# A fused attention and Hadamard-FFN block on one core: mixing W_down's blocks on GpSimd instead of TensorE, W_down loaded once, and new instruction orders

## The chip, the cores and the metric

One core of a Trainium2 chip. The metric is the device time of the whole kernel in microseconds (us), the median of several runs; lower is better.

## The reference, cut to what matters

The block runs over 8 sequences of 512 tokens and width 512. After the attention half comes a feed-forward half whose inputs are rotated by a Walsh-Hadamard transform (`fwht`) along the feature axis:

```python
x = x + layernorm(attention(layernorm(x)))       # 16 heads of 32, softmax, W_o
n = layernorm(x)
h = fwht(n * SU_ug) / 64                         # transform over 512
u = h @ W_up.T   * (Wscale_ug[:2048] * 64)
g = h @ W_gate.T * (Wscale_ug[2048:] * 64)
h = silu(g) * u
h = fwht(h * SU_dp) / 64                         # transform over 2048
x = x + layernorm(h @ W_down.T * (Wscale_dp * 64))
```

The transform is linear and symmetric, so it can be applied to the weights once instead of to the activations of every sequence. W_down is 512 x 2048, so its transform runs over 2048 = 16 blocks of 128. A Hadamard matrix of 2048 is one of 16 (it mixes the blocks, with signs) times one of 128 (it mixes inside a block).

## The kernel before

All matmuls are fp16 with each fp32 value split into a high and a low half; a product takes three passes (high-high, high-low, low-high). Work falls into three stages.

**Front.** Loads, the split of the attention weights (`asl`, `ash`), and the transform of the three FFN weights, interleaved with the attention of sequence 0 and part of that of sequence 1. **Steady cycle.** Six times the same list: the FFN of one sequence interleaved with the attention of the next. **Back.** What is left.

The order in each engine's queue is written out by hand-made lists: `FRONT` once and `ORDER` for each cycle, one string per engine (PE, ACT, DVE, POOL, SP). A token such as `smax.0.3` calls the function `smax` with those arguments; `@1` means for the next sequence, `@-1` for the one before. A planner wrote the lists; the hardware only sees the semaphore waits inside the functions. The work slots in PSUM (`MIDDLE`, `UPPER`) belong to the lists.

The steps that the change and the prediction touch, with their lines:

- SP: `ldx.k` (L573) loads 1 MB chunk k of W_down (k 0 to 3), W_up (4 to 7) and W_gate (8 to 11) to look for its largest value; `raw.k` (L586) loads the same chunk again to split it. `ln1.t` (L634) transposes token tile t of the normalized input, `stk` and `stq` (L656) the k and q tiles.
- DVE: `mx.k` takes the largest value of a chunk (L1150), `dmx`/`dsc` work out W_down's scale (`d_scaled`), `smax` takes the row maximum of scores (L1403).
- ACT: `ash` (L962, L964) scales and rounds attention weights, `cut.k` (L992, L1000) scales and rounds chunk k, `dyh`, `dzh`, `ue`, `uhh` copy PSUM results out, `exp`, `exr`, `exq` are the softmax exponentials.
- POOL: `asl` (L1482) and `cut.k` (L1486) subtract to get the low halves; `proj` and `tok` (L1504, L1509) finish the rotary embedding before `stk`; `xn` (L1498) the low half of the input.
- PE: `c`, `proj`, `v`, `smax`, `st`, `av`, `o` are the attention; `gate`, `up` (L913) and `down` (L938) the FFN; `warm.n` (L697) are n matmuls whose result nobody reads.
- The transform of W_down: `dy.n` (L738) transposes four blocks and sums them with signs (32 matmuls of 128 columns): the mixing over the low two bits of the block number. `dz.n` (L750, in `mixed`) multiplies by the 128-Hadamard and mixes over the high two bits: 4 blocks x 2 halves = 8 matmuls of 512 columns. There are 16 of each. `dyh`/`dyl` and `dzh`/`dzl` take the results out of PSUM, `dst` stores them.
- The transform of W_up and W_gate: `ut` (L764) and `uh` (L750), 32 of each.

The first `dy` waits for all four `cut` chunks: `pe.wait_ge(cut_lo, 4)`.

Of the kernel before, what the change touches and what calls it, by code (L numbers as in the profile page):

```python
# [44 lines left out]
ROW_SHIFT = 2.0 ** 12  # L45

# [15 lines left out]
        up.7@-1 smax.2.5 smax.2.6 gate.8@-1 smax.2.7 smax.2.8 smax.2.9 up.8@-1 st.22 gate.9@-1 st.23 smax.2.10  # L62
        av.2.0 proj.3.0 st.24 av.2.1 down.6@-1 st.25 down.7@-1 smax.2.11 smax.2.12 down.8@-1 smax.2.13 smax.2.14
        smax.2.15 up.9@-1 st.26 proj.3.1 st.27 gate.10@-1 up.10@-1 st.28 gate.11@-1 st.29 up.11@-1 gate.12@-1
        st.30 st.31 up.12@-1 st.32 av.3.0 av.3.1 st.33 down.9@-1 st.34 gate.13@-1 up.13@-1 st.35 st.36
        down.10@-1 smax.3.0 down.11@-1 st.37 st.38 gate.14@-1 up.14@-1 st.39 av.4.0 smax.3.1 smax.3.2 smax.3.3
        down.12@-1 smax.3.4 av.4.1 smax.3.5 c.1@1 gate.15@-1 st.40 smax.3.6 up.15@-1 c.0@1 down.13@-1 smax.3.7
        smax.3.8 down.14@-1 st.41 smax.3.9 smax.3.10 down.15@-1 st.42 smax.3.11 proj.0.0@1 gate.16@-1 st.43
        smax.3.12 smax.3.13 up.16@-1 smax.3.14 smax.3.15 gate.17@-1 proj.0.1@1 st.44 st.45 up.17@-1 gate.18@-1
        up.18@-1 st.46 gate.19@-1 st.47 up.19@-1 av.5.0 av.5.1 gate.20@-1 st.48 st.49 st.50 up.20@-1 gate.21@-1  # L70
        st.51 down.16@-1 down.17@-1 smax.0.0@1 smax.0.1@1 smax.0.2@1 up.21@-1 st.52 proj.1.0@1 smax.0.3@1
        smax.0.4@1 down.18@-1 down.19@-1 st.53 smax.0.5@1 smax.0.6@1 gate.22@-1 st.54 st.55 st.56 up.22@-1
        av.6.0 av.6.1 st.57 smax.0.7@1 down.20@-1 smax.0.8@1 down.21@-1 smax.0.9@1 smax.0.10@1 smax.0.11@1
        gate.23@-1 st.58 st.59 up.23@-1 gate.24@-1 st.60 up.24@-1 st.61 st.62 gate.25@-1 up.25@-1 proj.1.1@1
        st.63 av.7.0 down.22@-1 down.23@-1 smax.0.12@1 smax.0.13@1 gate.26@-1 smax.0.14@1 smax.0.15@1 down.24@-1
        av.7.1 v.0@1 v.1@1 up.26@-1 v.2@1 v.3@1 gate.27@-1 up.27@-1 st.0@1 st.1@1 gate.28@-1 up.28@-1 st.2@1
        down.25@-1 st.3@1 o.0 st.4@1 smax.1.0@1 gate.29@-1 o.1 st.5@1 up.29@-1 smax.1.1@1 smax.1.2@1 down.26@-1
        down.27@-1 o.2 smax.1.3@1 st.6@1 gate.30@-1 st.7@1 av.0.0@1 up.30@-1 proj.2.0@1 gate.31@-1 up.31@-1
        smax.1.4@1 smax.1.5@1 down.28@-1 av.0.1@1 smax.1.6@1 smax.1.7@1 smax.1.8@1 down.29@-1 o.3 down.30@-1
        down.31@-1 smax.1.9@1 smax.1.10@1 gate.0 up.0 gate.1 st.8@1 up.1 st.9@1 gate.2 smax.1.11@1 proj.2.1@1  # L80
        up.2 smax.1.12@1 st.10@1 smax.1.13@1 gate.3 up.3 st.11@1 smax.1.14@1 smax.1.15@1 down.0 st.12@1 st.13@1
# [1511 lines left out]
```

## Time and profile before

| what | us |
|---|---|
| median of 3 runs | 1946.56 (1945.4 to 1946.8) |
| the profiled execution | 1942.76 |
| its span, first to last instruction | 1940.8 |
| TensorE busy | 1842.3 (95%) |
| VectorE busy | 1276.8 (66%) |
| ScalarE busy | 1159.5 (60%) |
| GpSimd busy | 940.2 (48%) |
| mean granted TensorE clock | 0.991 of full |

Times in the views are from the start of the span. PE is TensorE, PEld its weight load, DVE VectorE, ACT ScalarE, POOL GpSimd, SPq the queue from which SyncE issues DMAs. A busy PE is not PE at its peak: the ends of matmuls are modelled and overlap the next ones, so the price of a group of matmuls is read from the starts, or from the chain.

### The profile page before, as it was taken

The page shows a single profiled execution, that of the slowest core. Times are in us where ns is not written, and L with a number is a line of the kernel's source. Part 1 is how long each engine was busy: PE and PEld are TensorE (multiplying, and loading weights), DVE is VectorE, ACT ScalarE, POOL GpSimd, SP SyncE. Part 2 cuts the span into 40 slices and gives each one's busy share as a digit, 9 for nine tenths or more (in the row PEclk, how much of TensorE's full clock was granted, in tenths as well). Part 3 has the DMA queues.
Part 4 walks back from the last instruction along what each step waited for, and adds up shares of the span by engine and source line. Part 5 has one row for each costly group of instructions (what it writes and reads, how often), then busy time and mean ns, then how long its engine had stood idle before and what let it go on. Part 6 is the DMA issues. An engine that isn't in the chain of part 4 may idle for free.

```text
span 1940.8 us, 46270 instructions
## 1 busy us (share of the span) xinstructions
PE 1842.3 (95%) x18248; PEld 1286.9 (66%) x18248; DVE 1276.8 (66%) x2669; ACT 1159.5 (60%) x2003; POOL 940.2 (48%) x990
## 2 busy tenths in 40 slices
PE   3699989999999999999999999999999999999998
PEld 1366555777667676767667776767677767777775
DVE  8788566776677766776677666776677666664322
ACT  3568998665647654666556564666457655664222
POOL 3624554464456444555456444545456445444322
PEclk9899999999999999999999999999999999999999
DMA  8745432463346325463455333543556334522422
GB/s 250 246 115 139 130 77 55 121 126 72 88 120 134 73 73 137 108 123 77 109 126 131 72 91 101 141 76 80 127 124 121 72 93 113 117 70 75 136 76 76
DMA packets 351959, 213.15 MB, mean 110 GB/s; under 512 B 284160, under 2 KB 285440, under 8 KB 350720
## 3 DMA queue, kind: packets, MB, share of 16 engines
q1 hardware_dynamic: 343536, 198.72, 43.1%
q10 hardware_dynamic: 8208, 11.48, 1.9%
q8 instruction: 146, 2.39, 0.5%
q14 instruction: 69, 0.57, 0.1%
HBM read 122.06 MB, written 20.98 MB: 74 GB/s over the span
## 4 chain that ended last, share of the span: by engine, by line
PE 76%; DVE 8%; ACT 5%; issue 4%; POOL 3%; DMA 2%; SPq 1%; POOLq 0%; ACTq 0%; DVEq 0%
PE ps L913 29%; PE ps L938 15%; PE ps L849 5%; PE ps L839 4%; PE ps L860 4%; PE ps L905 4%; PE ps L871 4%; PE ps L750 3%; DVE mx L1403 2%; PE ps L808 2%; PE ps L874 2%; ACT p_hi L1089 2%; POOL p_lo L1516 1%; PE ps L738 1%; PE ps L818 1%
## 5 line engine op out<-in xcount | busy, mean ns | idle before, releaser
L1089 ACT ACTIVATE p_hi<-ps,exp_scale 128x512 f16<-128x512 f32 x512 | 352.1, 688 | 232.1 <-PE ps L860 228.5
L1516 POOL TENSOR_TENSOR p_lo<-p,p_hi 128x512 f16<-128x512 f32 x256 | 296.5, 1158 | 259.5 <-ACT p L1095 246.0
L1403 DVE TENSOR_REDUCE mx<-ps 128x1 f32<-128x512 f32 x512 | 331.5, 684 | 120.3 <-PE ps L849 118.0
L913 PE MATMUL ps<-x2T,gate_w 128*128 128x256 f16 x3072 | 377.5, 273 | 8.5 <-DVE room L1451 8.4
L913 PE MATMUL ps<-x2T,up_w 128*128 128x256 f16 x3072 | 377.4, 273 | 0.0
L938 PE MATMUL ps<-room 128*128 128x512 f16 x1536 | 363.4, 379 | 0.1
L1544 POOL TENSOR_TENSOR room<-room 128x256 f16<-128x256 f32 x256 | 171.9, 672 | 380.5 <-ACT room L1125 379.1
L913 PEld LDWEIGHTS ps<-x2T,gate_w 128*128 128x128 f16 x3072 | 297.6, 98 | 67.1 <-DVE room L1451 14.8
L913 PEld LDWEIGHTS ps<-x2T,up_w 128*128 128x128 f16 x3072 | 299.1, 98 | 48.0 <-issue 3.0
L1418 DVE TENSOR_TENSOR p_lo<-ps,p_hi 128x512 f16<-128x512 f32 x256 | 175.8, 687 | 171.2 <-ACT ps L1100 99.6
L938 PEld LDWEIGHTS ps<-room 128*128 128x128 f16 x1536 | 148.2, 97 | 163.8 <-issue 3.0
L1120 ACT ACTIVATE room<-ps,half_gate 128x256 f32<-128x256 f32 x256 | 119.5, 473 | 154.8 <-PE ps L913 148.6
L1449 DVE SCALAR_TENSOR_TENSOR room<-room,ps 128x256 f32<-128x256 f32 x256 | 106.1, 414 | 153.0 <-ACT room L1120 152.2
L1095 ACT ACTIVATE p<-ps,exp_scale 128x512 f32<-128x512 f32 x256 | 176.2, 688 | 16.4 <-POOL p_lo L1516 16.4
L849 PE MATMUL ps<-kT,qT 96*128 96x512 f16 x512 | 163.8, 387 | 20.9 <-DVE mx L1403 7.0
L860 PE MATMUL ps<-qT,kT 128*128 128x256 f16 x1024 | 175.4, 273 | 5.2 <-DVE mx L1403 3.9
L1125 ACT ACTIVATE room<-room 128x256 f16<-128x256 f32 x256 | 105.1, 417 | 118.8 <-DVE room L1451 60.0
L1100 ACT ACTIVATE ps<-ps,exp_scale 128x512 f32<-128x512 f32 x256 | 169.7, 663 | 6.3
L860 PEld LDWEIGHTS ps<-qT,kT 128*128 128x128 f16 x1024 | 94.1, 98 | 48.4 <-DVE mx L1403 8.5
L1423 DVE RECIPROCAL nsc<-ps 128x256 f32<-128x256 f32 x64 | 112.0, 1750 | 21.1 <-PE ps L874 19.8
L1489 POOL TENSOR_TENSOR rs<-ve,mhalf 128x1 f32<-128x1 f32 x128 | 73.3, 576 | 94.2 <-DVE ve L1355 94.2
L1504 POOL TENSOR_TENSOR ra<-ra,rb 128x512 f32<-128x512 f32 x64 | 81.2, 1268 | 73.0 <-DVE rb L1394 58.2
(197 smaller groups left out, 2580.9 us busy)
## 6 DMA issues: line engine op xcount, KB each, us to landing
room<-down_mid SPq DMA_DIRECT2D x256, 256.0 KB, 3.0
xr<-in_x SPq DMA_DIRECT2D x34, 256.0 KB, 3.4
y_mid<-xr SPq DMA_DIRECT2D x32, 256.0 KB, 2.6
room<-y_mid ACTq DMA_DIRECT2D x32, 256.0 KB, 3.4
xa<-in_x SPq DMA_DIRECT2D x30, 256.0 KB, 3.2
out<-room SPq DMA_DIRECT2D x24, 256.0 KB, 2.1
x2T<-in_W_gate SPq DMA_DIRECT2D x5, 1024.0 KB, 6.1
gate_w<-in_W_down SPq DMA_DIRECT2D x4, 1024.0 KB, 7.1
```

Of the source, the lines that this page charges most:

```text
L849: nc.tensor.matmul(work[k], qT[0:STACK, g % 2, t, h, :], kT[0:STACK, g % 2, :, h, :], start=True, stop=True).then_inc(sm_filled.sem, 1)
L860: mm = nc.tensor.matmul(work[k][:, hh * HALF:(hh + 1) * HALF], kT[:, g % 2, kt, 2 * j + hh, :], qT[:, g % 2, 2 * qh:2 * qh + 2, 2 * j + hh ...
L913: mm = nc.tensor.matmul(ffn_ps[i % 2][:, half * HALF:(half + 1) * HALF], weights[:, chunks[j // 4], kt, pw, j % 4 * P:(j % 4 + 1) * P], x2 ...
L938: mm = nc.tensor.matmul(down_ps[t], hid[:, i % 2, ph, t * P:(t + 1) * P], wr[:, i % WB, pw, :], start=j == n == 0, stop=j == NJ - 1 and n ...
L1089: nc.scalar.activation(hi_buf(b, U)[:, 2 * j:2 * j + 2, :].rearrange("p h q -> p (h q)"), work[k], ACT.Exp, scale=exp_scale[:, 0:1]).then_ ...
L1095: nc.scalar.activation(p32[:], work[k], ACT.Exp, scale=exp_scale[:, 0:1]).then_inc(p_right.sem, 1)
L1100: nc.scalar.activation(work[k], work[k], ACT.Exp, scale=exp_scale[:, 0:1]).then_inc(p_left.sem, 1)
L1120: nc.scalar.activation(act[:, i % 2, :], ffn_ps[i % 2][:, 0:HALF], ACT.Tanh, scale=half_gate[:, 0:1]).then_inc(tanh_done.sem, 1)
L1403: nc.vector.tensor_reduce(mx[:, t, h:h + 1], work[k], AX.X, ALU.max).then_inc(sm_freed.sem, 1)
L1418: nc.vector.tensor_tensor(lo, work[k], hi, ALU.subtract).then_inc(st_freed.sem, 1)
L1516: nc.gpsimd.tensor_tensor(lo, p32[:], hi, ALU.subtract).then_inc(p_low.sem, 1)
L1544: nc.gpsimd.tensor_tensor(hid[:, i % 2, 1, :], act[:, i % 2, :], hid[:, i % 2, 0, :], ALU.subtract).then_inc(h_lo.sem, 1)
```

## The change

- The mixing over the high two bits of the block number is done by `bf.k` on GpSimd, in fp32, on the raw chunk as it was loaded: two butterfly steps over runs of 512 and 1024 columns, each one addition and one subtraction of 128 x 1024, out of place into `mid` and back. `dz` keeps only the 128-Hadamard: 2 matmuls in place of 8, and each `dz` needs only its own `dy`.
- W_down's chunks are loaded once, into the room of the later `up_w`; `mx` reads them there. `ldx.0` to `ldx.3` are gone. `bf.k` may overwrite the chunk only after `mx.k`.
- Two buffers of `raw`, `cut` and `turned` and their waits are rearranged, and all lists, `MIDDLE` and `UPPER` are written anew by the planner with other durations. The steady cycle is a rotation of the same tokens in a new order; `FRONT` ends a few tokens later.

```diff
+MIX = (4 * P, 8 * P)
...
-        RAW_AT = [gate_part(2), gate_part(0), gate_part(1), gate_part(2), gate_part(0), gate_part(2), gate_part(0), gate_part(2),
-                  x2_16, gate_part(0), x2_16, x2_16]
+        RAW_AT = [up_part(c) for c in range(4)] + [gate_part(0), x2_16, gate_part(0), x2_16, gate_part(0), x2_16, x2_16, x2_16]
+        mid = gate_part(3).bitcast(F32)
...
             def dz(b, n):
-                pe.wait_ge(t_done, 4 * (n // 4) + 4)
-                mixed(n, n % 4)
+                pe.wait_ge(t_done, n + 1)
+                if n == 0:
+                    pe.wait_ge(bo_sum, 2)
+                if n >= 2:
+                    pe.wait_ge(q_done, n - 1)
+                for i in range(2):
+                    mm = nc.tensor.matmul(ps[:, 6 + n % 2, :], had[0], d_turned[:, n % 2, i, :], start=i == 0, stop=i == 1)
+                mm.then_inc(q_filled, 1)
...
+            def bf(b, k):
+
+                pool.wait_ge(d_in[k], 16)
+                for n, width in enumerate(MIX):
+                    src, dst = ((raw[k], mid), (mid, raw[k]))[n % 2]
+                    left, right = (src.rearrange("p (m i n) -> p m i n", i=2, n=width)[:, :, i, :] for i in range(2))
+                    both = dst.rearrange("p (m i n) -> p m i n", i=2, n=width)
+                    if n == 0 and k:
+                        pool.wait_ge(d_mixed, k)
+                    if n:
+                        pool.wait_ge(d_turn, (len(MIX) - 1) * k + n)
+                    if n == 1:
+                        pool.wait_ge(m_seen, k + 1)
+                    nc.gpsimd.tensor_tensor(both[:, :, 0, :], left, right, ALU.add)
+                    nc.gpsimd.tensor_tensor(both[:, :, 1, :], left, right, ALU.subtract).then_inc(
+                        d_mixed if n == len(MIX) - 1 else d_turn, 1)
```

The `cut` of ScalarE waits for the mixing, and `dy` for the four W_down cuts under their own semaphore:

```diff
             def cut_(b, k):
-                sc.wait_ge(r_loaded[k % 3], 16 * (k // 3 + 1))
-                sc.wait_ge(d_scaled if k < 4 else f_scaled, 1)
+                if k < 4:
+                    sc.wait_ge(d_mixed, k + 1)
+                    sc.wait_ge(d_scaled, 1)
...
                 if n == 0:
-                    pe.wait_ge(cut_lo, 4)
+                    pe.wait_ge(d_lo, 4)
```

The beginning of three of the new lists, against the old (cut):

```diff
 FRONT POOL
-        xs.0 xs.1 xn.0 xs.2 xs.3 xn.1 xn.2 xn.3 asl.0 asl.1 asl.2 asl.3 asl.4 asl.5 asl.6 asl.7 asl.8 proj.0.0
-        asl.9 tok.0.0 asl.10 asl.11 proj.0.1 xs.0@1 tok.0.1 cut.0 proj.1.0 xs.1@1 tok.1.0 cut.1 cut.2 cut.3
+        xs.0 xs.1 xs.2 xn.0 xn.1 xs.3 bf.0 xn.2 bf.1 xn.3 asl.0 asl.1 asl.2 asl.3 asl.4 asl.5 asl.6 asl.7 asl.8
+        asl.9 bf.2 asl.10 asl.11 proj.0.0 cut.0 tok.0.0 xs.0@1 proj.0.1 cut.1 tok.0.1 bf.3 cut.2 proj.1.0 xs.1@1
+        cut.3 tok.1.0 proj.1.1 tok.1.1 low.0 low.1 low.2 low.3 low.4 proj.2.0 tok.2.0 low.5 xn.0@1 proj.2.1
 FRONT SP
-        xl.0 xl.1 xl.2 xl.3 lda.4 lda.2 ldv.2 lda.3 lda.1 lda.5 ldx.0 ldv.0 lda.0 ldx.1 ln1.0 xl.0@1 ln1.1 ldx.2
-        ln1.2 ln1.3 ldv.3 ldx.3 ldv.4 ldx.4 xl.1@1 rl.0 ldv.1 ldx.5 raw.0 wput.0 ldx.6 wget.0 raw.1 ldx.7 raw.2
-        stk.0.0 stk.0.1 ldx.8 raw.3 ldx.9 ldx.10 stq.0 stk.1.0 stk.1.1 ldx.11 wput.1 dst.0 dst.1 wget.1 raw.4
+        xl.0 xl.1 xl.2 lda.4 lda.2 ldv.2 lda.3 lda.1 xl.3 lda.5 ldv.0 raw.0 lda.0 raw.1 raw.2 raw.3 ldv.3 ldv.4
+        ldx.4 ldv.1 ldx.5 ln1.0 xl.0@1 ln1.1 ln1.2 ln1.3 wput.0 ldx.6 wget.0 rl.0 xl.1@1 ldx.7 ldx.8 ldx.9
+        ldx.10 stk.0.0 stk.0.1 ldx.11 stq.0 stk.1.0 stk.1.1 wput.1 dst.0 dst.1 wget.1 raw.4 raw.5 dst.2 dst.3
 FRONT PE
-        warm.10 dy.0 v.2 v.3 dy.1 st.0 st.1 dy.2 st.2 st.3 dy.3 st.4 st.5 smax.1.0 dy.4 smax.1.1 dz.0 smax.1.2
-        dy.5 smax.1.3 smax.1.4 dz.1 st.6 st.7 st.8 dy.6 av.0.0 smax.1.5 av.0.1 smax.1.6 st.9 dz.2 proj.2.0 dy.7
+        v.2 warm.10 dy.0 v.3 dy.1 st.0 st.1 dz.0 dy.2 dz.1 st.2 dy.3 dz.2 smax.1.0 dy.4 smax.1.1 smax.1.2 dz.3
+        st.3 dy.5 smax.1.3 smax.1.4 st.4 dz.4 st.5 st.6 dy.6 st.7 st.8 av.0.0 proj.2.0 av.0.1 dy.7 st.9 smax.1.5
```

## Rows read from the trace of the kernel before

**Rows 1.** The page: span, engines' busy time, granted clock by slice.

```profile
span 1940.8 us, 46270 instructions
...
PE 1842.3 (95%) x18248; PEld 1286.9 (66%) x18248; DVE 1276.8 (66%) x2669; ACT 1159.5 (60%) x2003; POOL 940.2 (48%) x990
...
PEclk9899999999999999999999999999999999999999
```

**Rows 2.** Windows: stretch, its length, busy time of each engine, clock, DMA.

```profile
0.00:98.02 98.02, 48.35 (x245) 24.59 (x246) 77.97 (x170) 43.97 (x50) 47.80 (x39) 0.88 0.83 247
98.02:226.00 127.98, 118.38 (x1456) 80.05 (x1454) 94.90 (x171) 101.51 (x148) 55.60 (x43) 0.99 0.52 133
226.00:348.50 122.50, 113.79 (x1028) 62.83 (x1027) 76.32 (x141) 107.54 (x156) 58.74 (x43) 0.99 0.32 75
...
400.00:1840.00 1440.00, 1418.87 (x14289) 1013.61 (x14288) 964.98 (x2038) 851.53 (x1541) 728.31 (x804) 1.00 0.45 104
1840.00:1940.80 100.80, 91.40 (x688) 66.80 (x686) 24.05 (x66) 22.79 (x51) 24.45 (x33) 0.98 0.27 79
```

**Rows 3.** Chain that ended last, start and length, first 114 us.

```profile
18.85 8.87 DMA xT<-nhl
27.80 0.64 ACT nhl L1050
...
28.51 1.16 POOL nhl L1498
29.69 0.35 SPq L621
30.16 3.39 DMA xT<-nhl
...
35.59 3.61 DMA xT<-nhl
...
39.29 5.29 PE ps L808 x12
...
48.26 0.73 ACT gate_w L962
49.01 0.63 ACT att_w L964
...
65.97 8.13 SPq L656
74.28 2.97 SPq L656
...
98.02 1.80 PE ps L738 x32
...
113.54 1.73 PE ps L750 x8
```

**Rows 4.** Windows, the stretch before the first transpose lands.

```profile
0.00:27.70 27.70, 0.91 (x4) 0.45 (x4) 20.57 (x51) 2.54 (x3) 5.52 (x12) 1.00 0.96 273
```

**Rows 5.** Groups by line, POOL, first 98 us: count, busy, mean ns, idle before.

```profile
L1486 POOL TENSOR_TENSOR up_w<-gate_w,up_w 128x2048 f16<-128x2048 f32 x4 | 16.2, 4071 | 5.4 <-ACT up_w L1000 5.4
L1482 POOL TENSOR_TENSOR att_w<-gate_w,att_w 128x512 f16<-128x512 f32 x12 | 14.1, 1181 | 6.1 <-ACT att_w L964 5.3
L1504 POOL TENSOR_TENSOR ra<-ra,rb 128x512 f32<-128x512 f32 x4 | 5.1, 1265 | 6.9 <-DVE rb L1394 6.9
```

**Rows 6.** Timeline, PE from 94 us: start, length.

```profile
94.61 0.39 PE L849 MATMUL ps<-kT,qT 96*128 96x512 f16 x1 [0.29 <-DVE mx L1403]
94.83 3.19 PE L697 MATMUL ps<-ident 128*128 128x512 f16 x14
```

**Rows 7.** The page: softmax exponentials and row maxima, mean ns of one after the busy time.

```profile
L1089 ACT ACTIVATE p_hi<-ps,exp_scale 128x512 f16<-128x512 f32 x512 | 352.1, 688 | 232.1 <-PE ps L860 228.5
```

**Rows 8.** Waits of PE, 400 to 1840 us: total, times, longest.

```profile
PE ps L913 <- DVE room L1451: 8.4, 12, 1.0
PE ps L849 <- DVE rb L1392: 6.0, 6, 1.0
```

More of the change, by code:

```diff
@@ L61 @@
     PE="""
[L62 to L81, printed above, removed]
@@ new lines @@
+        up.30@-1 st.6@1 st.7@1 o.2 av.0.0@1 down.27@-1 gate.31@-1 smax.1.5@1 smax.1.6@1 up.31@-1 av.0.1@1 o.3
+        st.8@1 down.28@-1 down.29@-1 proj.2.1@1 down.30@-1 down.31@-1 st.9@1 smax.1.7@1 gate.0 up.0 gate.1 up.1
+        smax.1.8@1 smax.1.9@1 smax.1.10@1 gate.2 smax.1.11@1 smax.1.12@1 up.2 gate.3 smax.1.13@1 smax.1.14@1
+        smax.1.15@1 up.3 st.10@1 st.11@1 down.0 st.12@1 down.1 st.13@1 st.14@1 gate.4 up.4 st.15@1 down.2
+        av.1.0@1 av.1.1@1 st.16@1 gate.5 st.17@1 st.18@1 up.5 gate.6 st.19@1 down.3 st.20@1 up.6 gate.7
@@ L137 @@
+        hid.31@-1 o.3 fs.2@-1 fs.3@-1 fe.2@-1 hid.0 hid.1 ys.2 low.4@1 fe.3@-1 proj.2.1@1 low.5@1 hid.2 low.6@1
+        low.7@1 norm.0@1 tok.2.1@1 oe.3 hid.3 low.8@1
     """,
     SP="""
-        xl.0@1 stq.1 xl.1@1 stk.2.0 stk.2.1 wl.5@-1 wl.6@-1 wl.7@-1 wl.8@-1 ln2.2@-1 ln1.0@1 wl.9@-1 xl.2@1
-        wl.10@-1 wl.11@-1 wl.12@-1 oe.3@-1 stq.2 ln1.1@1 xl.3@1 stk.3.0 stk.3.1 ln1.2@1 wl.13@-1 wl.14@-1
-        wl.15@-1 ln1.3@1 ln2.3@-1 wl.16@-1 wl.17@-1 stq.3 stk.0.0@1 wl.18@-1 wl.19@-1 stk.0.1@1 wl.20@-1
@@ L191 @@
-        down.4 smax.2.1@1 gate.7 down.5 smax.2.2@1 smax.2.3@1 smax.2.4@1
+        aturn.0 aback.0 bos aturn.1 aback.1 warm.7 warm.7 c.1 c.0 proj.0.0 warm.7 warm.7 proj.0.1 v.0 v.1
+        proj.1.0 warm.3 warm.3 warm.3 smax.0.0 smax.0.1 smax.0.2 smax.0.3 smax.0.4 smax.0.5 smax.0.6 warm.5
+        smax.0.7 smax.0.8 smax.0.9 warm.4 smax.0.10 smax.0.11 smax.0.12 smax.0.13 smax.0.14 smax.0.15 proj.1.1
+        v.2 warm.10 dy.0 v.3 dy.1 st.0 st.1 dz.0 dy.2 dz.1 st.2 dy.3 dz.2 smax.1.0 dy.4 smax.1.1 smax.1.2 dz.3
@@ L192 @@
+        up.10 down.7 st.27@1 st.28@1 gate.11 st.29@1 proj.3.1@1 up.11 down.8 down.9 st.30@1 st.31@1 st.32@1
+        gate.12 av.3.0@1 st.33@1
     """,
     ACT="""
[L194 to L197 removed]
@@ L244 @@
+        low.7@1 yn.2 gelu.4 norm.1@1 low.8@1 gelu.5 low.9@1 low.10@1 smax.2.0@1 gelu.6
     """,
     POOL="""
[L246 to L249 removed]
@@ L256 @@
+        low.18 low.19 tok.0.0@1 cut.7 cut.8 norm.3 low.20 low.21 low.22 low.23 proj.0.1@1 cut.9 tok.0.1@1 low.24
+        proj.1.0@1 norm.4 low.25 low.26 tok.1.0@1 low.27 norm.5 cut.10 norm.6 low.28 low.29 low.30 low.31
+        proj.1.1@1 cut.11 norm.7 tok.1.1@1 o.0 o.1 oe.0 ys.0 low.0@1 oe.1 low.1@1 low.2@1 ys.1 yn.0 low.3@1 yn.1
+        proj.2.0@1 o.2 o.3 tok.2.0@1 hid.0 oe.2 oe.3 proj.2.1@1 low.4@1 hid.1 low.5@1 low.6@1 norm.0@1 ys.2
+        hid.2 low.7@1 tok.2.1@1 hid.3 low.8@1
     """,
@@ L265 @@
+        xl.3@1 dst.11 dst.12 raw.7 ln1.2@1 ln1.3@1 dst.13 stq.2 stk.3.0 dst.14 stk.3.1 raw.8 dst.15 raw.9 stq.3
+        stk.0.0@1 stk.0.1@1 raw.10 raw.11 stq.0@1 stk.1.0@1 stk.1.1@1 oe.0 ln2.0 rl.2 oe.1 rl.3 ln2.1 oe.2 wl.0
+        wl.1 wl.2 wl.3 stq.1@1 stk.2.0@1 wl.4
     """,
@@ L503, in program @@
         d_scaled, f_scaled = sem("d_scaled"), sem("f_scaled")
+        d_in, d_turn, d_mixed, d_lo = [sem(f"d_in{k}") for k in range(4)], sem("d_turn"), sem("d_mixed"), sem("d_lo")
         xb_in = [sem(f"xb_in{k}") for k in range(2)]
@@ L1554, in fe @@
                 nc.gpsimd.tensor_tensor(yt[:, k, :], yt[:, k, :], ft, ALU.add).then_inc(fin_done.sem, 1)
-            run(pool, "POOL", dict(asl=asl, cut=cut_, xs=xs, xn=xn, proj=proj, tok=tok_, low=low, norm=norm, o=o, oe=oe, ys=ys, yn=yn, hid=hid_, fs=fs, fe=fe))
+            run(pool, "POOL", dict(asl=asl, bf=bf, cut=cut_, xs=xs, xn=xn, proj=proj, tok=tok_, low=low, norm=norm, o=o, oe=oe, ys=ys, yn=yn, hid=hid_, fs=fs, fe=fe))
 _PRE = {"x": "L0_attn_x"} | {n: "L0_attn_" + n for n in (
```

376 lines of the change are left out of this document (197 added, 179 removed), and 10 rows, old and new, of tables (MIDDLE, UPPER).

## The prediction

> **What bounds the kernel now.** I read the page first: TensorE is busy 1842.3 of 1940.8 us at almost the full clock [rows 1]. The kernel lasts as long as TensorE's work plus its gaps, so the gaps have to be placed. The windows do that [rows 2]. Three stretches matter. Until 98.02 us, where the first `dy` starts, TensorE is busy 48.35 us, much of it `warm` matmuls: it waits for the loads and the first attention steps. From 98.02 to 348.5, where the first `gate` starts, it is busy 118.38 + 113.79 = 232.17 of 250.48 us: 18.3 us of gaps. From 348.5 to the end it is busy but for 21.1 us of gaps between 400 and 1840 and 9.4 in the back. So 98 us of gaps in all, half of them in the first 98 us, and little to be had in the steady cycle: its largest waits, for the activation and for the row maxima, are 8.4 and 6.0 us, each made of pieces of at most 1.0 [rows 8].
>
> Two more things in the same windows. In the first stretch the DMA engines are 83% busy, and the chain lies on DMA there: the first transpose takes 8.87 us from its issue to its end, the next, with a shorter queue ahead, 3.39; later a transpose holds the SP queue for 8.13 us [rows 3]. In the middle ScalarE is busy 107.54 of 122.5 us (88%) [rows 2], close behind TensorE. What TensorE loses in work there ScalarE may not be able to follow.
>
> **The change part by part.**
>
> *The blocks' mixing leaves TensorE.* 16 `dz` lose 6 of 8 matmuls, 96 in all. Eight cost 1.73 us in the chain [rows 3], 0.216 each: 96 x 0.216 = 20.7 us of TensorE work less. `dy` and the ScalarE, VectorE copies keep their number.
>
> *The mixing comes to GpSimd.* Each of four `bf` has four two-input instructions of 128 x 1024 fp32. The trace has 512 columns in 1.18 us (fp16 out) and 1.27 (fp32 out), and 2048 in 4.07 [rows 5]. Below, one costs half of 4.07, 2.04; above, two of 1.27, 2.53. The line through 1.18 and 4.07 gives 2.14 at 1024; fp32 output adds the 0.08 between 1.27 and 1.18. I take 2.2: 8.8 us for a `bf`, bounds 8.2 and 10.1, 35 us for all. The Trainium skill (GPSIMD Engine Reference, Elementwise — side-by-side cycle accounting) gives 4497 ns for a two-input fp32 instruction of 2048 columns, by which a `bf` would be an estimated 9.0 us and the three on the path below 0.6 us longer in all; the same page (Engine selection) would keep such work off GpSimd, as about twice slower than VectorE. What decides here is where the 35 us lie.
>
> *W_down is loaded once.* 4 MB less, but the four chunks, and `ldx.4` and `ldx.5`, are now queued ahead of `ln1.0`. Before, what was issued ahead of `ln1.0` was about 6.75 MB (x 1, attention weights 3, biases 0.75, two chunks), and the transpose ended at 18.85 + 8.87 = 27.7 [rows 3]; these 27.7 us ran at 273 GB/s with the engines 96% busy [rows 4]. Four chunks more go ahead now: 4 x 1.05 MB / 0.273 = 15.4 us; by the other count, 27.7 less the 3.4 of a short transpose over 6.75, 3.6 us each, 14.4. `ln1.0` then ends at about 42 instead of 27.7 (39 to 43). That it doesn't overtake is what the 8.87 against 3.39 shows. The Trainium skill (DMA: Bandwidth & Descriptors, Queues, rings and completion order) says the same, that an engine takes descriptors in ring order; if it were not so, this term would be nothing.
>
> *What follows on GpSimd.* `xn.2` needs the landing, a ScalarE rounding 0.64 and 1.16 on GpSimd [rows 3]: done at 44.1. `bf.0` fits ahead of it, its chunk being there at about 24. Then, in the order of the list, with 1.18 for `asl` and `xn`, 1.27 for `proj`, 1.2 for `tok`, 4.07 for `cut` and 0.6 for a root: `bf.1` to 52.9, `xn.3` 54.1, ten `asl` 65.9, `bf.2` 74.7, two `asl` 77.1, `proj.0.0` 78.3, `cut.0` 82.4, `tok.0.0` 83.6, root and `proj.0.1` 85.5, `cut.1` 89.6, `tok.0.1` 90.8. The last goes to `stk.0.1` and 4 us later to the first `smax`: about 94.8, where it was 78.7. The rest: `bf.3` 99.6, `cut.2` 103.7, `proj.1.0` and a root 105.5, `cut.3` 109.6. The other engines keep up with this. The six `ash` ahead of `xn.3` on ScalarE take 6 x 1.4 (0.73 and 0.63 with their gaps [rows 3]) after 42.7 and are done at 51; 16 `smax` at 0.62 and a statistics step bring the row maxima to about 106, then `proj.1.1`, `v.2` and `warm.10` (14 such matmuls took 3.19 [rows 6]) bring TensorE to 110. Both ways the first `dy` starts near 110.3 instead of 98.0: **12.3 us late**. Bounds: with 8.2 for a `bf` and a landing at 39, 7.5; with 10.1 and 43, 17.
>
> *The front from `dy.0` to the first `gate`.* By a count of the two lists TensorE's work there falls by 20.7, by `v.2` (0.65, now ahead of `dy.0`) and by four `smax` (4 x 0.216, now behind the `gate`) to 210.0 us. ScalarE loses four exponentials at 0.69 [rows 7], 209.05 - 2.8 = 206.3. So neither engine alone sets the end. If TensorE keeps its 18.3 us of gaps the stretch is 228.3. If ScalarE is as busy as in its fuller half, 88%, it is 235.0. I take the middle, 231.7: **18.8 us less** than 250.5, with 0.9 given back behind the first `gate`. Bounds 22.2 and, if ScalarE only reaches the mean 83% of before (209.05 of 250.48), 3.3.
>
> *The new orders.* The steady cycle's tokens are the same, so only the 21.1 us of gaps can change. I take no change; below it can't gain more than 21, realistically 10; above, nothing in the trace bounds a worse order, and I take 10 as well. The 4 MB less of loading beyond `ln1` I cost at nothing: from 98 us on DMA is at most 52% busy [rows 2].
>
> The sum against the profiled execution: its span 1940.8 + 12.3 - 18.8 + 0.9 = 1935.2, and with the 1.96 around the span 1937.2 for 1942.76. The median of the runs lies 3.8 above that execution: 1941.0.
>
> **The rivals.**
>
> *The late start is hidden.* If the transposes pass the queued chunks, or if GpSimd's list has more slack than I give it, `dy.0` starts near 98 and the whole saving stays: 1941.0 - 12.3 = 1929. For it: the lists were planned anew around just this. Against it: GpSimd alone has 65 us of work without a gap between 44 and 110 in my count, and the loads ahead of it are a matter of bytes.
>
> *ScalarE takes TensorE's place* (the other side). Its exponentials and the copies of `dy`, `dz`, `ut` and `uh` don't get fewer, and it was already 88% busy from 226 to 348.5. If it stays at the 83% of the whole stretch, that takes 206.3 / 0.835 = 247.2, the saving is 3.3, and 1946.6 + 12.3 - 3.3 + 0.9 = 1956.5. It turns from gain to loss where the stretch takes more than 237.3 us (250.5 - 12.3 - 0.9), ScalarE at 87%. For it: the saved work lies in the half in which ScalarE is only 101.5 of 128 us busy, and once 20.7 are gone the two are equal. Against it: in that half there is this room.
>
> *The steady order decides.* Every cycle runs six times, so 1.7 us more or less in each gives 10: 1931 or 1951. For it: the gaps are 1.5% and all small, easy to lose. Against it: a queue that is over 98% busy leaves little to gain.
>
> *The change does not cut TensorE's path at all*, because `dz` was hidden: excluded, the `dz` groups stand in the chain one after another.
>
> **How the numbers follow.** My forecast has 0.41 (1935 to 1947 as its own range), the hidden start 0.20 (1929), ScalarE's bound 0.20 (1956), the steady order better 0.08 (1931) and worse 0.11 (1951). A measurement of this kernel can tell 0.2%, 3.9 us, from no change: faster is under 1942.7, slower over 1950.5. From the forecast 0.26 is faster, 0.14 same, 0.01 slower; with the rest, faster 0.53, same 0.18, slower 0.29. The range for 8 in 10 goes from 1927 to 1956. The likeliest time is 1941.
>
> **What the next profile would show.** `bf` as 16 POOL instructions of 128 x 1024, near 2.2 us. The first transpose ending near 42. The first `smax` near 95 and the first `dy` near 110. `dz` as groups of 2 matmuls. The first `gate` near 342 (110.3 + 231.7), ScalarE near 89% busy in between. The steady gaps near 1.5%. The prediction is wrong if the first `dy` is within 5 us of 98, if the stretch from there to the first `gate` is over 240 us or under 226, or if the steady cycle shows other gaps.

## The result, and the profile after

The changed kernel takes 1950.96 us (median of 11 runs, 1949.44 to 1952.35) against 1946.3 for the kernel before in the same runs: ratio 1.0025, 95% interval 1.0016 to 1.0034, so slower, by about 4.7 us. I had forecast 1941, 5.6 us faster. The profiled execution has a span of 1947.6 us, 6.8 more than before. The page:

```profile
span 1947.6 us, 46102 instructions
...
PE 1830.5 (94%) x18152; PEld 1279.9 (66%) x18152; DVE 1273.5 (65%) x2669; ACT 1158.8 (59%) x2003; POOL 976.9 (50%) x1006
...
PEclk9689989999999999999999999999999999999999
```

The 96 matmuls are gone (18248 to 18152) and GpSimd has its 16 instructions more; yet TensorE's busy time fell by 11.8 us only, and the clock line has a 6 in the second slice, where it had an 8 [rows 1]. The windows, cut at the first `dy` (121.60) and the first `gate` (371.90):

```profile
0.00:121.60 121.60, 51.49 (x246) 23.85 (x247) 91.68 (x163) 43.87 (x50) 84.39 (x54) 0.80 0.62 172
121.60:371.90 250.30, 219.11 (x2380) 134.72 (x2379) 171.77 (x316) 208.51 (x301) 114.29 (x85) 0.95 0.40 98
371.90:1947.60 1575.70, 1559.94 (x15529) 1121.38 (x15527) 1010.01 (x2191) 906.38 (x1652) 778.23 (x868) 1.00 0.43 104
```

Set against [rows 2], the 6.8 us are three terms. The first `dy` is 23.6 us later (98.0 to 121.6). The stretch from there to the first `gate` is 0.2 shorter (250.5 to 250.3). What follows is 16.7 shorter (1592.4 to 1575.7). 23.6 - 0.2 - 16.7 = 6.7, the 6.8 but for rounding. I had 12.3, -18.8 and 0.9: no term held.

**The start.** The chain of what ended last:

```profile
19.63 13.08 SPq L564
...
33.85 3.98 SPq L579
...
38.04 6.41 DMA xT<-nhl
44.53 0.63 ACT nhl L1074
...
64.11 7.01 DMA oT<-in_W_up
71.14 2.29 DVE room L1174
...
74.71 1.71 DVE room L1325
76.44 2.27 DVE room L1326
...
82.60 1.27 POOL ra L1548
...
83.93 4.06 POOL gate_w L1513
87.99 1.12 POOL tok L1553
```

The SP queue holds for 13.08 us on a small load behind the four chunks, then 3.98 on `ldx.5`, and the first transpose is issued at 38.04 and ends at 44.45; I had 42. Then the chain leaves what I had followed. It goes to `ldx.6` (7.01 us), its largest value on VectorE, W_down's scale, whose steps stand ahead of `proj.0.0` in VectorE's list, and on to `cut.0`, which stands ahead of `tok.0.0` on GpSimd. GpSimd's timeline beside it:

```profile
45.24 1.16 POOL L1542 TENSOR_TENSOR nhl<-xr,nhl 128x512 f16<-128x512 f32 x1 [10.85 <-ACT nhl L1074]
46.35 2.35 POOL L1528 TENSOR_TENSOR gate_w<-up_w 128x1024 f32<-128x1024 f32 x1
48.66 2.35 POOL L1529 TENSOR_TENSOR gate_w<-up_w 128x1024 f32<-128x1024 f32 x1
51.10 2.35 POOL L1528 TENSOR_TENSOR up_w<-gate_w 128x1024 f32<-128x1024 f32 x1
53.40 2.34 POOL L1529 TENSOR_TENSOR up_w<-gate_w 128x1024 f32<-128x1024 f32 x1
...
56.82 12.52 POOL L1509 TENSOR_TENSOR att_w<-gate_w,att_w 128x512 f16<-128x512 f32 x10
...
114.89 4.06 POOL L1513 TENSOR_TENSOR up_w<-up_w 128x2048 f16<-128x2048 f32 x1 [0.46 <-ACT up_w L1019]
```

One `bf` is 9.4 us (2.35 each; I had 2.2 and 8.8). GpSimd is nearly without a gap from 45 to 112, so here my reading of it as a full queue looks right. It isn't the whole of it: its gaps of 1.69, 1.35 and 1.90 us before `proj.0.0`, `proj.0.1` and the root behind `proj.1.0` are waits for VectorE, and the experiments show more. The first `smax` starts at 102.4 (I had 94.8), `cut.3` ends at 118.95 (109.6).

On VectorE, two one-column instructions beside `bf.2`:

```profile
74.71 1.70 DVE L1325 TENSOR_TENSOR room<-room 128x1 f32<-128x1 f32 x1
76.44 2.26 DVE L1326 TENSOR_TENSOR room<-room 128x1 f32<-128x1 f32 x1
```

They took 0.94 and 0.16 before; the last section comes back to why.

**The middle.** TensorE's counted work fell to 210.0 (206.8 is what e15 below shows at a clock of 0.99), but it is busy 219.1: 9 to 12 us are matmuls at the lower clock. Five windows of 2.5 us:

```profile
244.10:246.60 2.50, 2.48 (x39) 1.45 (x37) 1.36 (x2) 2.29 (x3) 1.35 (x1) 1.00 0.00 0
246.60:249.10 2.50, 1.26 (x5) 0.19 (x2) 2.41 (x5) 2.47 (x4) 2.50 (x1) 1.00 0.00 0
249.10:251.60 2.50, 1.84 (x5) 0.35 (x5) 2.42 (x5) 2.50 (x4) 1.87 (x2) 0.54 0.42 75
251.60:254.10 2.50, 2.50 (x9) 1.14 (x9) 2.14 (x4) 2.50 (x6) 2.50 (x2) 0.50 0.90 342
254.10:256.60 2.50, 2.50 (x9) 0.94 (x7) 0.00 (x0) 1.36 (x3) 1.69 (x2) 0.60 0.01 2
```

TensorE is half idle, waiting for row maxima; then the granted clock is half, the 1.2 GHz level, and 16 matmuls of 512 columns from 252.61 on take 5.36 us (0.335 each, part of them already behind the clock's rise) where eight take 1.73 (0.216) before [rows 3]. Of such windows 12 of 101 are under 0.9 in this stretch, before 4 of 101. And TensorE's own waits there rose from 17.4 us in all to 30.0: for VectorE from 12.0 to 21.3, for ScalarE from 4.5 to 7.8. The saved 20.7 us turned into waits and slower matmuls.

**The steady cycle.** The waits of TensorE from 400 to 1840 us:

```profile
PE ps L921 <- DVE room L1478: 2.4, 6, 0.4
PE ps L868 <- DVE p_lo L1445: 2.4, 6, 0.4
```

These two are all that the view lists. Before, 8.4 and 6.0 [rows 8] and two more, 3.5 for the row maxima and 2.3 for GpSimd: 20.2 in all against 4.8.

### The profile page after: what moved, and what is told of

Its sections match the earlier page's. It is cut to its first block, busy times and chain, and to the rows that moved or that the text cites. A ratio compares the mean times of both kernels' runs of the same rounds, so it can differ in the third digit from the quotient of the medians.

```text
span 1947.6 us, 46102 instructions
## 1 busy us (share of the span) xinstructions
PE 1830.5 (94%) x18152; PEld 1279.9 (66%) x18152; DVE 1273.5 (65%) x2669; ACT 1158.8 (59%) x2003; POOL 976.9 (50%) x1006
## 4 chain that ended last, share of the span: by engine, by line
PE 86%; DVE 6%; ACT 2%; issue 2%; SPq 2%; DMA 1%; POOL 0%; POOLq 0%; ACTq 0%; DVEq 0%
PE ps L921 34%; PE ps L946 16%; PE ps L857 5%; PE ps L868 5%; PE ps L847 5%; PE ps L879 5%; PE ps L913 4%; PE ps L882 3%; PE ps L752 3%; DVE mx L1430 2%; PE ps L816 2%; PE ps L826 1%; PE ps L743 1%; PE ps L839 1%; SPq L564 1%
## 5 line engine op out<-in xcount | busy, mean ns | idle before, releaser
L1113 ACT ACTIVATE p_hi<-ps,exp_scale 128x512 f16<-128x512 f32 x512 | 352.2, 688 | 242.9 <-PE ps L868 237.7
L868 PE MATMUL ps<-qT,kT 128*128 128x256 f16 x1024 | 177.6, 275 | 11.4 <-DVE p_lo L1445 4.7
L868 PEld LDWEIGHTS ps<-qT,kT 128*128 128x128 f16 x1024 | 94.8, 98 | 68.3 <-DVE mx L1430 11.2
L1548 POOL TENSOR_TENSOR ra<-ra,rb 128x512 f32<-128x512 f32 x64 | 81.2, 1268 | 111.5 <-DVE rb L1421 97.1
L1533 POOL TENSOR_TENSOR rs<-ve,mhalf 128x1 f32<-128x1 f32 x128 | 71.4, 561 | 95.1 <-DVE ve L1382 94.8
```

Source lines behind the costliest of these rows:

```text
L868: mm = nc.tensor.matmul(work[k][:, hh * HALF:(hh + 1) * HALF], kT[:, g % 2, kt, 2 * j + hh, :], qT[:, g % 2, 2 * qh:2 * qh + 2, 2 * j + hh ...
L1113: nc.scalar.activation(hi_buf(b, U)[:, 2 * j:2 * j + 2, :].rearrange("p h q -> p (h q)"), work[k], ACT.Exp, scale=exp_scale[:, 0:1]).then_ ...
```

## The experiments

Before's median beside the runs lay between 1945.5 and 1946.7; ratios are to it, with 95% intervals. "Start" is the first `dy`, "middle" the stretch to the first `gate`, "rest" what follows.

| run | median us | ratio | start | middle | rest |
|---|---|---|---|---|---|
| before | 1946.3 | | 98.0 | 250.5 | 1592.4 |
| after | 1950.96 | 1.0025 (1.0016 to 1.0034) | 121.6 | 250.3 | 1575.7 |
| e1 | 1927.64 | 0.9904 (0.9889 to 0.9918) | 101.8 | 250.3 | 1575.0 |
| e2 | 1974.29 | 1.0142 (1.0126 to 1.0159) | 119.8 | 257.1 | 1594.8 |
| e3 | 1944.72 | 0.9993 (0.9984 to 1.0002) | 102.4 | 250.1 | 1593.1 |
| e4 | 1960.32 | 1.0074 (1.0059 to 1.0089) | 123.8 | 259.3 | 1575.7 |
| e5 | 1947.23 | 1.0006 (0.9997 to 1.0016) | 119.1 | 250.4 | 1575.7 |
| e6 | 1950.05 | 1.0019 (1.001 to 1.0029) | 122.4 | 250.7 | 1575.6 |
| e7 | 1964.63 | 1.0097 (1.0082 to 1.0112) | 136.3 | 250.2 | 1575.7 |
| e8 | 1945.19 | 0.9999 (0.999 to 1.0008) | 101.8 | 249.8 | 1592.2 |
| e9 | 1951.74 | 1.0036 (1.0022 to 1.005) | 124.0 | 250.2 | 1575.7 |
| e10 | 1956.19 | 1.0056 (1.0043 to 1.0068) | 127.0 | 253.9 | 1575.7 |
| e11 | 1938.05 | 0.9965 (0.9953 to 0.9978) | 107.1 | 250.7 | 1575.7 |
| e12 | 1941.94 | 0.9983 (0.9975 to 0.9992) | 124.3 | 242.9 | 1576.0 |
| e13 | 1946.86 | 1.0009 (1.0 to 1.0018) | 121.1 | 249.1 | 1574.7 |
| e14 | 1948.98 | 1.0016 (1.0007 to 1.0024) | 122.9 | 248.9 | 1574.8 |
| e15 | 1927.64 | 0.9909 (0.9896 to 0.9923) | 121.2 | 227.0 | 1574.8 |
| e16 | 1942.05 | 0.9979 (0.997 to 0.9988) | 123.4 | 243.3 | 1574.7 |

The start is read from one execution each and varies: with the unchanged front it is 98.0 in before, and 101.8, 102.4 and 101.8 in e1, e3 and e8. Differences of the start of up to 4.4 us say nothing by themselves; the medians, over several executions, help out. The middle repeats within 0.5 us where nothing in it is changed, but for e10, whose 253.9 (3.6 longer) has no cause that a run here shows.

### e1 and e2: the steady orders apart from the front

e1 keeps the kernel before with its front (mixing on TensorE) and takes only the new steady lists and their slots; e2 is the reverse.

```diff
-ORDER, MIDDLE, UPPER of before
+ORDER, MIDDLE, UPPER of after; FRONT of before, prolonged by the tokens up to where the new cycle begins
```

> The kernel before (W_down mixed on TensorE, loaded twice, old front lists) with only the steady lists and their work slots of the changed kernel; the old front is prolonged by the tokens that the new one has behind it. Theory that the parts are separate: the 14.8 us fewer TensorE gaps behind the first gate come from the new steady order alone, so the time is about 1946.3 - 15 = 1931, and the stretch from the first gate to the end about 1576 us. Rival: the front of the changed kernel has only taken over waits from the cycle (copies and exponentials are further ahead when the cycle begins), so an old front gives it back: 1943 to 1947.

> The changed kernel's front (mixing on GpSimd, one load, its lists up to the first gate) with the old steady lists and slots. Separate parts: the first gate near 372 us as in the changed kernel, from there 1592 as in the kernel before, 1951 + 15 = 1966 in all. Rival, as above: near 1951.

e1 gains 18.7 us (0.0096 x 1946.7), e2 loses 27.6. Together that is a loss of 8.9, after's own is 4.7 to 4.9. The difference of 4 fits into the 6.8 us by which e2's middle is longer than after's, where its front's tokens were spliced to the old cycle. So the parts add up, and the new steady orders alone are the gain:

```profile
101.80:352.10 250.30, 231.99 (x2483) 143.13 (x2481) 171.16 (x312) 208.98 (x303) 114.30 (x86) 0.99 0.44 105
352.10:1927.10 1575.00, 1559.39 (x15528) 1120.86 (x15524) 1010.15 (x2189) 904.72 (x1650) 776.47 (x865) 1.00 0.43 103
```

Behind the first `gate`, 15.6 us of gaps (1575.0 - 1559.4). e1 is the fastest kernel measured that computes everything: it beats both.

### e3, e8, e4: what TensorE's saved work is worth in the middle

e3 is before with only two of the eight `dz` matmuls; it leaves out six of eight terms of each sum. e8 also narrows ScalarE's first pass of `cut.4` to `cut.11` to 64 columns. e4 is after with its two `dz` matmuls issued four times.

```diff
 # e3
-                    for i in range(2):            # for each of 4 blocks
+                    (one block of the four only)
 # e4
-                for i in range(2):
+                for m in range(4):
+                    for i in range(2):
```

> The kernel before with nothing but the mixing over the high two block bits left out: dz does 2 of its 8 matmuls (so W_down's transform is not the reference's). 20.7 us of TensorE work less, nothing else moved. If TensorE sets the pace between the first dy and the first gate: 1946.3 - 18 = 1928 (1926 to 1931). If ScalarE and the chains through it do, as the 83% suggests: no better than 1941.

> The kernel before with dz at 2 of 8 matmuls, as in the earlier run that brought nothing, and ScalarE's first pass over the eight chunks of W_up and W_gate cut to 64 columns of 512 or 2048 (their scaling is left out but for that): 16 us of ScalarE work less, in instructions on which no matmul waits directly. If ScalarE's amount of work sets the stretch from the first dy to the first gate: 250 falls to 236 and the time to 1931. If the stretch is set by the hand-overs between TensorE, ScalarE and VectorE in list order, each with its latency: less than 5 us, 1940 or more.

> The changed kernel with 8 matmuls in every dz again, the same block four times (output not the reference's): TensorE's 20.7 us given back, all else as changed. If TensorE set the pace there: 1951 + 19 = 1970. If it has 31 us of gaps because others set it: 1951 to 1957. The granted clock of the stretch was 0.95 with the gaps; if it goes back to 0.99 with the dummy work, that is 9 us of the extra cost undone, and the time can stay at 1951.

e3's middle:

```profile
102.40:352.50 250.10, 216.63 (x2387) 135.79 (x2385) 170.95 (x312) 208.78 (x303) 114.37 (x86) 0.97 0.42 105
```

In the old lists, then, 20.7 us of TensorE work less shorten the stretch by 0.4: TensorE is busy 15.5 less (not 20.7: its clock is 0.97 for 0.99) and idle 15.2 more. The medians agree: the ratio makes it 1.4 us, and at most 3.1 by its interval. Whoever took `dz` for TensorE's critical work because its groups stand in the chain, as I did, finds it free here. With 11.4 us less of ScalarE as well (e8), still nothing: 249.8. In the new lists the same 20.7 us cost 9.0 (e4: 250.3 to 259.3), all of it by `st.31`, in the half with `dy` and `dz` (9.9 there).

### e12 to e16: who holds TensorE

e12 narrows ScalarE's copies in after (`dyh`, `dzh` from the third, `ue` from the third group, first pass of `cut.4` to `cut.11`), e14 VectorE's row maxima, e13 those and VectorE's low halves (`dyl`, `dzl`, and `low`; `uhl` stayed whole, against what its expectation says), e15 is e12 and e13 together, e16 is e15 with the `dz` of e4. All leave out most of the numbers they narrow.

```diff
 # e12
-  nc.scalar.activation(d_turned[:, n % 2, 0, :], ps[:, 5, :], ACT.Copy)
+  w = 512 if n < 2 else 64
+  nc.scalar.activation(d_turned[:, n % 2, 0, 0:w], ps[:, 5, 0:w], ACT.Copy)
 # e13, e14
-  nc.vector.tensor_reduce(mx[:, t, h:h + 1], work[k], AX.X, ALU.max)
+  nc.vector.tensor_reduce(mx[:, t, h:h + 1], work[k][:, 0:64], AX.X, ALU.max)   # in the front, from the second group
```

> The changed kernel with ScalarE's copies out of PSUM for the weight transforms (dyh and dzh from the third on, ue from the third group on) and the first pass of cut.4 to cut.11 cut to 64 columns; this leaves out most of their numbers. It takes about 45 to 50 of ScalarE's 208.5 us between the first dy and the first gate. Theory 'ScalarE's amount of work sets the new middle stretch' (my rival of 247.2 us): 250.3 falls to what TensorE needs, 219.1 and some 10 of gaps, about 230, and the median to about 1931. Rival 'TensorE is held by hand-overs that VectorE, DMA and the order set': it falls by under 5 us, 1946 to 1951. The start (first dy near 121.6) and the steady cycle stay.

> The changed kernel with VectorE's row maxima (from the second head group on), its low halves of the exponentials (from the fifth unit on) and its low halves of the weight transforms (dyl, dzl, uhl from the third on) taken over 64 of 512 columns, in the hand-made list of the front alone; this leaves out most of those numbers. It takes some 90 of VectorE's 171.8 us between the first dy and the first gate. There TensorE waits 21.3 us for VectorE, 7.8 for ScalarE. Theory 'TensorE is held by hand-overs from VectorE': 250.3 falls by 12 to 20, to 230 to 238, and the median to about 1935. Rival 'ScalarE, whose chain of exponentials and copies is the next thing': it falls by under 8, 1943 to 1951.

> Of that only the row maxima, over 64 of 512 columns, in the front from the second head group on. The score matmuls wait for these 6.3 us as matmuls and 12.8 us as weight loads. If this one hand-over is most of VectorE's share, the stretch falls by 8 to 12 us; if it is one of several, by 2 to 5.

> The run with less of VectorE together with the run with less of ScalarE. If the two together were what stood between the saved TensorE work and the end, the stretch falls to TensorE's 210.0 us of work and under 12 of gaps, to 215 to 225, and the median to about 1920. If what remains is TensorE's own order of dependent steps with DMAs between, it stays above 230.

> The run with less of VectorE and of ScalarE, and in it dz with eight matmuls of the same block, so TensorE's 96 matmuls of 0.216 us are back and the mixing on GpSimd stays. If the two engines were all that kept the saved work from counting, the stretch from the first dy to the first gate is now 20.7 us longer than without, 227.0 to about 247.7, against 9.0 where the two engines are loaded in full, and the median is about 1948. If TensorE's work is worth half in any case, it is about 236 and 1937.

The middle of e12, of e13, of e15 and of e16:

```profile
124.30:367.20 242.90, 216.90 (x2380) 135.40 (x2379) 168.59 (x315) 168.80 (x301) 114.21 (x85) 0.96 0.42 100
```

```profile
121.10:370.20 249.10, 215.43 (x2381) 135.49 (x2380) 119.21 (x316) 208.35 (x301) 114.36 (x86) 0.96 0.40 98
```

```profile
121.20:348.20 227.00, 206.78 (x2380) 132.54 (x2379) 114.05 (x316) 167.90 (x301) 114.25 (x85) 0.99 0.45 108
```

```profile
123.40:366.70 243.30, 227.34 (x2476) 143.36 (x2475) 116.16 (x315) 168.32 (x301) 114.34 (x86) 0.99 0.43 100
```

Forty us off ScalarE (208.5 to 168.8) bring 7.4. Fifty-two off VectorE (171.8 to 119.2) bring 1.2, and the row maxima alone (142.3 busy) 1.4. Both together bring 23.3, nearly three times the sum. Each is read from one execution; by the ratios of the medians the three are 8.2, 3.1 and 22.6 us, twice the sum, so that it is more than the sum stands and the factor is loose. Of the 23.3, TensorE's gaps are 11.0 (31.2 to 20.2) and its shorter busy time 12.3 (219.1 to 206.8, the clock 0.99 for 0.95); with ScalarE alone relieved the two are 5.2 and 2.2, with VectorE alone the gaps grow by 2.5 and the busy time falls by 3.7. So my theory of the VectorE hand-overs fell (12 to 20 expected), and that of ScalarE's amount of work too (20 expected): each engine's relief only uncovers the other. In e13 TensorE's waits for VectorE fall from 21.3 to 16.1 us and those for ScalarE rise from 7.8 to 14.9; in e15 they are 8.4 and 10.6. And only with both relieved is TensorE's work worth most of its price: 96 matmuls more (227.34 - 206.78 = 20.6 us busy) lengthen the stretch by 16.3 (13.6 by the medians' ratios), not 9.0.

### e5, e6, e7: one suspect of the late start at a time

e5 narrows the mixing to 4 columns of each run, so its result isn't the transform's. e6 issues `ln1.0` behind two chunks, and `ln1.1`, `ln1.2` ahead of `ldx.4`. e7 puts `bf` on VectorE.

```diff
 # e5
-  nc.gpsimd.tensor_tensor(both[:, :, 0, :], left, right, ALU.add)
+  nc.gpsimd.tensor_tensor(both[:, :, 0, 0:4], left[:, :, 0:4], right[:, :, 0:4], ALU.add)
 # e6, SP
-  raw.1 raw.2 raw.3 ldv.3 ldv.4 ldx.4 ldv.1 ldx.5 ln1.0 xl.0@1 ln1.1 ln1.2 ln1.3
+  raw.1 ln1.0 raw.2 raw.3 ldv.3 ldv.4 xl.0@1 ln1.1 ln1.2 ldx.4 ldv.1 ldx.5 ln1.3
```

> The changed kernel with each of the 16 mixing instructions on GpSimd cut to 4 columns per run (the mixing is left out but for that); loads, waits and lists stay. If the late start is GpSimd's queue: the three bf behind xn.2 cost 28 us on its path, and VectorE's one-column additions that took 1.70 and 2.26 us beside a bf fall to 0.2; the first dy goes from 121.6 to 98 to 101, the time from 1951 to about 1929. If it is the loads queued ahead of the first transpose, which ended at 44.5 instead of 27.7: the first dy stays over 112 and the time over 1941.

> The changed kernel with one change in SP's list: ln1.0 is issued behind raw.1, ln1.1 and ln1.2 ahead of ldx.4. The first transpose should end near 31 instead of 44.5. If the landing starts GpSimd's chain: xn.2 on GpSimd ends at 35.6 instead of 46.4 (bf.0 runs until 34.4), all behind it comes 10.8 us sooner, first dy at 111, time 1941. If GpSimd's own amount of work or another engine sets the start: first dy within 3 us of 121.6 and 1949 to 1951.

> The changed kernel with the same 16 mixing instructions on VectorE (bf.0 behind asc, bf.1 behind asd, bf.2 behind mx.4, bf.3 behind proj.0.0), all else as changed. I expect 1.15 us each, 18 in all on an engine that is busy 91.6 of 121.6 us there, and GpSimd free of 37.6: first dy at 108 to 112, time about 1940. Rival: VectorE becomes the bound of the start (its scale chains asc, asd and dsc come behind the mixing), first dy no earlier than 121, time 1951 or more.

e5's timeline of GpSimd:

```profile
45.45 1.16 POOL L1542 TENSOR_TENSOR nhl<-xr,nhl 128x512 f16<-128x512 f32 x1 [15.18 <-ACT nhl L1074]
...
53.60 1.16 POOL L1542 TENSOR_TENSOR nhl<-xr,nhl 128x512 f16<-128x512 f32 x1 [6.15 <-ACT nhl L1074]
...
79.67 1.26 POOL L1548 TENSOR_TENSOR ra<-ra,rb 128x512 f32<-128x512 f32 x1 [9.45 <-DVE rb L1421]
```

34.5 us of GpSimd's work are gone (84.4 to 49.9 ahead of the first `dy`), and GpSimd waits in their place; `proj.0.0` is at 79.67 instead of 82.60, the first `dy` 2.5 us earlier, less than the start varies; the medians say 3.7. In e6 the first transpose's low half ends on GpSimd at 36.2 instead of 46.4, and the first `smax` is 1.4 us earlier, the first `dy` not at all: GpSimd then waits 6.7 us for `mx.1` on VectorE, which must have read the chunk before `bf.1` overwrites it, and 3.9 for the rotary products behind W_down's scale there. Each suspect alone is nearly free. e7 answers where the mixing should go if not there: VectorE is then busy 110.9 instead of 91.7 us in the start, the first `smax` is at 116.8, and 13.7 us are lost against after. VectorE's sixteen mixing instructions took 28.9 us in all, where at the 1.22 of those that ran undisturbed (last section) they would take 19.5, so the run doesn't show what the amount of work alone costs there.

### e9, e10, e11: the lists' order and the mixing together

e9 has e6's loads, `xn.3` ahead of the first six `ash`, and the first `proj` and `tok` ahead of W_down's scale and cuts on all engines. e10 also moves the mixing on GpSimd, from `bf.1` on, behind them. e11 is e10 with e5's narrow mixing.

```diff
 # e9, DVE
-  c.1 mx.6 c.0 dsc proj.0.0 mx.7 mx.8 proj.0.1
+  c.1 c.0 proj.0.0 dsc mx.6 mx.7 proj.0.1 mx.8
 # e10, POOL
-  bf.0 xn.2 bf.1 xn.3 asl.0 ... asl.9 bf.2 asl.10 asl.11 proj.0.0 cut.0 tok.0.0 xs.0@1 proj.0.1 cut.1 tok.0.1 bf.3
+  bf.0 xn.2 xn.3 asl.0 ... asl.11 proj.0.0 tok.0.0 bf.1 xs.0@1 proj.0.1 tok.0.1 bf.2 cut.0 cut.1 bf.3
```

> The changed kernel with only its lists' beginning reordered; every instruction stays. The first transpose goes out behind two chunks instead of four, the rounding of the fourth token tile goes ahead of the first six attention weights on ScalarE, and the first rotary products (proj.0.0, tok.0.0, proj.0.1, tok.0.1) go ahead of W_down's scale on VectorE and of the first cuts on ScalarE and GpSimd. Theory 'the lists' beginning is late by its order': proj.0.0 ends on GpSimd near 73 instead of 83.9 (c.0 is on VectorE at 74 only since the loads and the six weights delay c), tok.0.1 near 90 instead of 97.4, first smax near 94 instead of 102.4, first dy near 113 instead of 121.6, median about 1942. Rival 'GpSimd's amount of work': between the first transpose and cut.3 GpSimd still has all 38 us of mixing and four cuts of 4.06 us, so cut.3 stays near 118 and the first dy near 120, though smax is earlier; median 1948 to 1951. The stretch from the first dy to the first gate stays at 250.3 in both.

> The kernel of the run before (attention's first steps ahead), and the mixing moved on GpSimd too: bf.1 behind tok.0.0, bf.2 behind tok.0.1, instead of ahead of xn.3 and amid the asl. Same instructions. Theory 'order': c starts near 48 (60.1 in the changed kernel), first smax near 80 as in the kernel before. GpSimd has from 45 on two xn, twelve asl, proj and tok twice, three bf of 9.4, four cut of 4.06, about 67 us without a wait, so cut.3 ends near 114 and the first dy starts near 115: here the amount of work on GpSimd sets it; median about 1944. Rival 'loads and hand-overs': GpSimd waits in between as in the run with the tiny mixing (15 and 9 us), cut.3 stays near 119 and the first dy near 121; median about 1950.

> The lists of the run before with the mixing cut to 4 of 512 (1024) columns, so that its result is not the transform's. It leaves out about 34 us of GpSimd's work. If the lists' order held the start back and GpSimd's work is what is left then, the first dy falls by some 12 to 15 us against the run before, to about 100, where the kernel before has it, and the median to about 1930. If hand-overs between the engines hold it back in any order, it moves by 2 to 3 us only, as in the run with the tiny mixing alone (121.6 to 119.1).

The start of e10 and of e11:

```profile
0.00:127.00 127.00, 50.55 (x246) 24.76 (x246) 85.83 (x167) 43.84 (x50) 82.27 (x54) 0.85 0.61 169
```

```profile
0.00:107.10 107.10, 49.06 (x246) 22.50 (x247) 77.76 (x167) 43.88 (x50) 48.27 (x54) 0.89 0.71 200
```

e10 brings the first `smax` from 102.4 to 92.7, and still the first `dy` is at 127.0: what was won is given back in `bf.2`, the cuts and `bf.3`, one after another on GpSimd from 83.8 to 126.9 with 6.5 us of waits, all for ScalarE's half of the cuts between them. Without the mixing the same lists reach 107.1, 19.9 us earlier, while in after's own lists the mixing is worth 2.5 (e5). With the mixing the better order is worth nothing (121.6 to 124.0 and 127.0), without it 12.0 (119.1 to 107.1). These are single executions, and e11's was the fastest of its five, e10's the slowest: the medians of the two lie 18.1 us apart, 3.2 of them in the middle, so the 19.9 is 15 to 20, and the 12.0 is 8 to 12. The pattern stays. The late start has two causes side by side, each hiding the other, as in the middle. Five to nine us of 107.1 against before's 98.0 to 102.4 stay without a cause of their own.

## Why the prediction was wrong, point by point

**"12.3 us late"**: the mechanism was there, the size was not. 23.6 measured, beyond my bound of 17; 19 to 24 by the spread of the unchanged start. The mixing was 2.35 us an instruction, which makes three `bf` on the path 1.8 longer, and the transpose was 2.4 later than 42 (44.45, outside my 39 to 43); together those 4 would have stayed within 17. They put GpSimd's last `asl` at 80.9 for my 77.1. The failed step is "The other engines keep up with this", which had every wait of GpSimd and TensorE for VectorE at nothing. From there to the end of `cut.3` GpSimd waits 5.4 us, 4.9 of them for VectorE, first behind W_down's scale (chain: 71.14 to 81.2), so that `proj.0.0` is at 82.60. TensorE's first `smax` comes 5.0 us after `tok.0.1`, not 4, behind `mx.9` and `v` on VectorE, and the row maxima wait for `mx.10` (2.3 us) ahead of them there: they end at 116.8 for my 106. That makes 7.6 us late at the first `smax` and 11.3 at the first `dy`. And e5 shows that the path over VectorE alone, without GpSimd's load, ends at 119. I followed one engine's list where two paths were nearly equally long.

**"18.8 us less" in the middle**: the mechanism was wrong. 0.2 measured. The failed step is "If TensorE keeps its 18.3 us of gaps": the saved matmuls are gone, but I let TensorE keep its gaps on the one side and ScalarE its busy share of the fuller half, 88%, on the other. Neither holds: the gaps rose to 31.2, and ScalarE's share came out at 83.3%, which looks like my rival (247.2 us). That rival is refuted as a matter of ScalarE's amount of work by e8 and e12. What the runs showed in its place: VectorE and ScalarE take turns in holding TensorE, and relief counts when both have it (e15, 227.0, close to my 228.3 for kept gaps). Whether other lists for this stretch could cash the saving with both engines fully loaded wasn't tried. The clock adds to it: a less occupied TensorE had its slow pieces more often (0.95 for 0.99, 9 to 12 us of longer matmuls). How far the clock is cause and how far consequence wasn't tried.

**The new orders, "I take no change"**: -16.7, more than the 10 that I called realistic, within the 21.1 that I had read as the most. e1 shows that it is the steady lists and nothing else. The row was there: the waits of [rows 8] and two more add up to 20.2 of the 21.1 us of gaps, that is, the gaps were waits in list order and not a floor. I had also read the second of them wrongly: its 6.0 us are score matmuls that wait until VectorE has read the rotary products (`rb`) out of PSUM; for the row maxima it is 3.5.

**The hidden start** didn't come. **"The change does not cut TensorE's path at all"** I had excluded, "the `dz` groups stand in the chain one after another". e3 shows the opposite: in the old lists `dz` is worth 0.4 us. Being in the chain means that nothing else was late at that moment; it doesn't say that something else isn't late 1 us after.

The sum was saved from a larger miss by errors of opposite sign: 11.3 too little at the start, 18.6 too much in the middle, 16.7 not counted in the cycle, 0.9 too much behind the `gate`: 11.3 + 18.6 - 16.7 - 0.9 = 12.3, against a span 12.4 over my 1935.2.

## What to carry to other kernels

Before work is taken off the fullest engine, ask for each stretch which other engines it waits for and add those waits up; where two others hold it in turn, taking work from it, or from one of them, is worth a fraction (here 0.4 to 9.0 of 20.7 us), and only relief of both brings out most of its price (14 to 16). Work that is put on an idle engine in a stretch that another path already bounds looks nearly free in a test that takes it away alone (2.5 us) and costs several times as much (15 to 20) once the other path is mended: take both away before calling either free. Price an order by its waits, and measure it apart from the change that it comes with: here the orders alone gain 0.96%, and the change that they came with more than ate it.
